# Row maxima from four partial products, two heads side by side in row groups of TensorE

## The reference, cut to what matters

```python
x_h = x.reshape(b, t, h, d).transpose(0, 2, 1, 3)            # 16, 16 heads, 512, 8
xw = jnp.einsum('bhtd,hde->bhte', x_h, w_att_val)
att = jnp.einsum('bhte,bhse->bhts', xw, x_h) / jnp.sqrt(jnp.asarray(d, x.dtype))
att = jax.nn.softmax(att, axis=-1)
vx = x @ wv_w.T + wv_b
...
o = jnp.einsum('bhts,bhsd->bhtd', att, vx)
return o @ out_w.T + out_b
```

## Time and profile before

| | us |
|---|---|
| median of 3 runs | 3337.77 (3323.8 to 3337.84) |
| the profiled execution | 3341.8 |
| its span | 3340.0 |
| PE, DVE, ACT, POOL busy | 3107.4, 2437.6, 2328.8, 1226.7 |

### The profile page before, as it was taken

How to read it: one execution, slowest core, us unless ns; L and a number is a source line. 1 busy time by engine, 2 the same in 40 slices (tenths; PEclk the granted TensorE clock), 3 DMA queues, 4 the chain that set the end, 5 groups by cost and what they waited for, 6 DMA issues and landing times.

```text
span 3340.0 us, 84102 instructions
## 1 busy us (share of the span) xinstructions
PE 3107.4 (93%) x34202; PEld 1889.6 (57%) x34202; DVE 2437.6 (73%) x4967; ACT 2328.8 (70%) x4800; POOL 1226.7 (37%) x778
## 2 busy tenths in 40 slices
PE   5899799999999999999999999999999999999976
PEld 5288446555565656465555656565555556565644
DVE  6722578878787868788787878788787878787643
ACT  4452376877777777868777776778787777777754
POOL 1133043444333333434433332434444333333433
PEclk9699699999999999999999999999999999999988
DMA  5356101011010111110100101111100101010000
GB/s 142 113 153 170 38 28 35 26 30 33 14 42 24 36 32 35 28 35 25 35 18 24 42 24 35 28 35 32 35 26 17 37 24 42 24 35 29 8 10 4
DMA packets 128413, 133.98 MB, mean 40 GB/s; under 512 B 18004, under 2 KB 110910, under 8 KB 128030
## 3 DMA queue, kind: packets, MB, share of 16 engines
q1 hardware_dynamic: 123488, 119.29, 12.9%
q0 software_dynamic: 4544, 9.32, 1.3%
HBM read 80.98 MB, written 30.28 MB: 33 GB/s over the span
## 4 chain that ended last, share of the span: by engine, by line
PE 65%; DVE 14%; ACT 7%; issue 3%; POOL 1%; DMA 1%; SPq 0%; POOLq 0%; ACTq 0%
PE bank L1456 7%; PE bank L2018 7%; PE bank L724 6%; PE bank L1469 6%; PE bank L1440 5%; PE bank L2062 3%; PE bank L2004 3%; PE bank L1994 3%; PE bank L1975 3%; PE bank L1960 2%; PE bank L1985 2%; PE bank L1717 2%; PE bank L2068 2%; DVE turn_f L2191 2%; PE bank L1735 2%
## 5 line engine op out<-in xcount | busy, mean ns | idle before, releaser
L1525 ACT ACTIVATE prob_a<-bank 128x512 f32<-128x512 f32 x1024 | 558.5, 605 | 132.0 <-PE bank L1469 129.4
L1580 DVE TENSOR_REDUCE nmax_a<-bank 128x1 f32<-128x512 f32 x768 | 496.8, 684 | 48.8 <-PE bank L1440 45.4
L1927 POOL TENSOR_TENSOR rn<-ss,minus_half 128x16 f32<-128x16 f32 x128 | 393.6, 3075 | 281.9 <-DVE ss L2186 278.7
L1950 POOL TENSOR_TENSOR rs_f<-rs_f,minus_half 128x4 f32<-128x4 f32 x32 | 33.0, 1032 | 1052.2 <-DVE rs_f L1320 1052.2
L1933 POOL TENSOR_TENSOR turn_f<-turn_f 128x512 f32<-128x512 f32 x256 | 325.3, 1291 | 203.1 <-DVE turn_f L2191 203.1
L2080 ACT ACTIVATE area<-bank 128x512 f32<-128x512 f32 x640 | 350.4, 603 | 55.7 <-PE bank L2018 46.3
L1469 PE MATMUL bank<-Qst_a,Kst_a 74*128 74x512 bf16 x1024 | 370.1, 386 | 9.3 <-DVE nmax_a L1580 5.8
L2191 DVE TENSOR_TENSOR turn_f<-area,rotf 128x1024 f32<-128x1024 f32 x256 | 303.7, 1218 | 7.8 <-POOL area L1937 6.8
L1440 PE MATMUL bank<-Kst_a,Qst_a 72*128 72x512 bf16 x768 | 298.6, 389 | 10.6 <-ACT prob_a L1525 6.2
L1456 PE MATMUL bank<-prob_a,V_a 128*9 128x512 f32 x2048 | 272.8, 605 | 18.1 <-ACT prob_a L1525 17.8
L1937 POOL TENSOR_TENSOR area<-turn_f,rn 128x1024 f32<-128x1024 f32 x128 | 243.9, 1905 | 18.4
(11 more groups left out here) (301 smaller groups left out, 6973.0 us busy)
## 6 DMA issues: line engine op xcount, KB each, us to landing
Qst_a<-dq_a SPq DMA_DIRECT2D x192, 96.0 KB
Kst_a<-dk_a SPq DMA_DIRECT2D x192, 96.0 KB
area<-in_W SPq DMA_DIRECT2D x25, 512.0 KB, 4.9
dq_a<-prob_a SPq DMA_DIRECT2D x80, 128.0 KB
V_f<-in_W SPq DMA_DIRECT2D x14, 512.0 KB, 4.5
dk_a<-prob_a SPq DMA_DIRECT2D x48, 128.0 KB
ys_d<-otok_f SPq DMA_DIRECT2D x39, 128.0 KB, 3.5
x_a<-in_x_in SPq DMA_DIRECT2D x16, 256.0 KB, 2.9
```

What stands on the lines that cost most here:

```text
L1525: nc.scalar.activation(dst, bk.full(act, product)[0:rows, :], func, **kw).then_inc(a_emptied["act"], 1)
L1580: nc.vector.tensor_reduce(out=nmax_a[:, g, t, j:j + 1], in_=bk.full(dve, f)[:], op=ALU.max, axis=AX.X, negate=True).then_inc(emptied, 1)
L1927: nc.gpsimd.tensor_tensor(rn[:, t % 2], ss[:, t % 2], minus_half[:], ALU.pow).then_inc(f_root, 1)
```

## The change

The first pass takes four of the nine partial products: the query's parts (1, 0, 0, 1) with the key's parts (0, 1, 0, 1), 4 x 8 = 32 rows. A stack `Qmx_a`, `Kmx_a` of its own holds the four heads of a group in four row groups of 32 partitions. `greatest` makes a head's product from its row group, and the products of two heads of the same quarter follow each other on PE, into two banks. The second pass keeps its 74 rows. To have the needed order of parts in DRAM, the spill writes 7 + 5 parts instead of 5 + 3; a stack is loaded by 8 DMAs instead of 6, two of 128 KB and six of 96 KB. The maxima's buffers become a ring of two, `mT_a` lies in unused rows of `Qst_a`, and four constants of the routing lie in buffers that are used later. The tables and the seats are all new.

```diff
+MT = 96
+Q_PARTS, K_PARTS = (1, 0, 0, 1, 2, 0, 1), (0, 1, 0, 1, 2)
...
-STEP = 178.7555
+STEP = 179.6323333
...
-        Kst_a, Qst_a = sb("Kst_a", [ROWS, RING, 4, T], BF16), sb("Qst_a", [ROWS, RING, 4, T], BF16)
+        Kst_a, Qst_a = sb("Kst_a", [ROWS, RING, 4, T], BF16), sb("Qst_a", [P, RING, 4, T], BF16)
+        Kmx_a, Qmx_a = sb("Kmx_a", [P, RING, T], BF16), sb("Qmx_a", [P, RING, T], BF16)
...
-        mhi_a, mT_a = sb("mhi_a", [P, G, NT, 4], BF16), sb("mT_a", [8, 2, T], BF16)
+        nmax_a, mparts_a = sb("nmax_a", [P, 2, NT, 4]), sb("mparts_a", [P, 2, NT, 2, 4])
+        mhi_a, mT_a = sb("mhi_a", [P, 2, NT, 4], BF16), Qst_a[MT:MT + 8, 0, 0:2, :]
...
-        first = [[("first", g, j, t) for j in range(4) for t in range(NT)] for g in range(G)]
+        first = [[("first", g, j, t) for t in range(NT) for j in range(4)] for g in range(G)]
...
-            for c in range(2 * SPLIT - 1):
-                sp.dma_start(dq[:, c], parts_q[:, c % SPLIT, :]).then_inc(s, 16)
-                if c < SPLIT:
-                    sp.dma_start(dk[:, c], parts_k[:, c, :]).then_inc(s, 16)
+            for c, part in enumerate(Q_PARTS):
+                sp.dma_start(dq[:, c], parts_q[:, part, :]).then_inc(s, 16)
+                if c < len(K_PARTS):
+                    sp.dma_start(dk[:, c], parts_k[:, K_PARTS[c], :]).then_inc(s, 16)
...
+            sp.dma_start(Qmx, dq[h:h + n, 0:4].rearrange("h c d t -> h (c d) t")).then_inc(s, 16)
+            sp.dma_start(Kmx, dk[h:h + n, 0:4].rearrange("h c d t -> h (c d) t")).then_inc(s, 16)
             rows = SPLIT * D0
-            q_rows, k_rows = (d[h:h + n].rearrange("h c d t -> (c d) h t") for d in (dq, dk))
+            q_rows, k_rows = (d[h:h + n, 2:].rearrange("h c d t -> (c d) h t") for d in (dq, dk))
...
+        def greatest(pe, bk, f):
+            _, g, j, t = f
+            rows = slice(32 * j, 32 * j + 32)
+            nc.tensor.matmul(bk.take(pe, f)[:], Qmx_a[rows, g % RING, t * P:(t + 1) * P],
+                             Kmx_a[rows, g % RING, :], start=True, stop=True).then_inc(a_filled, 1)
...
-                _, _, j, t = f = first[g][n]
                 if n == 0:
                     pe.wait_ge(*nth(r, a_stack[g], STACKED))
-                nc.tensor.matmul(bk.take(pe, f)[:], Qst_a[0:STACK, g % RING, j, t * P:(t + 1) * P],
-                                 Kst_a[0:STACK, g % RING, j, :], start=True, stop=True).then_inc(a_filled, 1)
+                for f in first[g][n:n + 2]:
+                    greatest(pe, bk, f)
```

More of the change, by code:

```diff
@@ L85 @@
                       314, 318.9, 323.8, 328.7, 333.6, 368.1),
[L86 to L92, removed]
+                     (-580.59649, -580.59449, -579.7103, -577.23387, -527.32015, -404.94056, -375.4343,
+                      -369.76896, 75.73973, 224.54907, 261.49146, 354.09913, 528.94049, 644.78191, 743.39294,
+                      842.14194, 907.68533, 1118.09809, 1131.5059, 1431.14303, 1431.14503, 1478.95922,
+                      1633.30607, 1659.50634, 1729.02134, 1732.58592, 1792.05439, 1792.15046, 1825.62492,
+                      1835.36098, 1849.53219, 1894.01227, 1915.99599, 1918.43704, 1929.50758, 1945.61039,
+                      1998.2619, 2003.15702, 2031.07034, 2071.21309, 2112.26554, 2133.72636, 2273.51371,
+                      2635.52919, 2639.14204, 2796.35045, 2864.13346, 4450.21639)),
             "head": ((1, 2),
-                     (94.66748, 95.66748))},
+                     (-257.83784, -256.83784))},
         "tensor": {
@@ L276 @@
                    17.8, 18.4, 18.8, 19.8, 23, 24),
[5 rows of a table removed]
-            "head": ((4.5, 6, 16, 16.7, 17.4, 18.1, 18.8, 19.5, 20.2, 20.9, 21.6, 22.3, 23, 23.7, 24.4, 25.1,
[4 rows of a table removed]
[5 rows of a table added]
+            "head": ((4.5, 6, 16, 17.4, 18.8, 20.2, 21.6, 23, 24.4, 25.8, 29),
[2 rows of a table added]
             "f": ((1, 1.3, 1.6, 6.4, 6.7, 7, 11, 11.2, 11.8, 12.1, 12.4, 13, 16.4, 16.5, 16.6, 16.8, 17.2,
@@ L424 @@
                    98.4, 99.6, 100.8, 102, 103.5, 105, 111),
[10 rows of a table removed]
[10 rows of a table added]
             "feed": ((6.55, 6.8, 7.1, 8.8, 9.3, 9.8, 10.725),
-                     (-112.76509, -111.65438, -110.77237, -103.08967, -101.79345, -99.4833, -77.78949)),
+                     (-110.64419, -110.64219, -109.49393, -102.26616, -99.67783, -95.92056, -78.05479)),
             "finish": ((13.2, 13.4, 13.6),
-                       (-58.22573, -55.4072, -53.6288))}}
+                       (-59.03677, -58.89768, -56.87055))}}
 SEATS = {
-    "a": ("154203542054415324103240512302323013124514003554035030102035022530543105243150130531013001"
-          "4532011520531051023103150350342"),
-    "b": "550243503111500034533453305032530452",
-    "head": "32010321541515105430",
-    "f": ("321401341540154325031214124541423451224254512415544510520151430123510545402503420312434212"
-          "4312012042141403"),
-    "feed": "433230540"}
+    "a": ("054132541354143251033504123003413054450230150440150122302414202014420325412305434035430410"
+          "4325142354530242105310210354410"),
+    "b": "525014251201105020322030345030052242",
+    "head": "12345034251432410244",
+    "f": ("351210451524013210142324355153521045121251224531441132103313510334530545243512543034030454"
+          "1254154011252523"),
+    "feed": "532523521"}
 B_AT = 5
@@ L749, in mixer_kernel @@
         turned_x = [hT_f[:], hT[:]]
-        tri, part_off = sb("tri", [P, P], BF16), sb("part_off", [P, 1])
-        block_at, ones_sq = sb("block_at", [P, NBLK]), sb("ones_sq", [P, P], BF16)
+        tri, part_off = gate_b[:].rearrange("p t g h -> p (t g h)")[:, 0:P // 2].bitcast(BF16), sb("part_off", [P, 1])
+        block_at, ones_sq = pool_b[:, 0:NBLK], gate_b[:].rearrange("p t g h -> p (t g h)")[:, P // 2:P].bitcast(BF16)
         m_stats = spare_b[:, 0:192].rearrange("p (g t s) -> p g t s", g=4, s=6)
@@ L943, in ranks @@
                 ps, first = rank_bank(c), 16 * c
-                nc.tensor.matmul(ps, tri[:], hot_bf[:, first:first + 16, :], start=True, stop=False, skip_group_check=True)
+                nc.tensor.matmul(ps, tri, hot_bf[:, first:first + 16, :], start=True, stop=False, skip_group_check=True)
                 for m in range(15):
-                    last = nc.tensor.matmul(ps[:, NX * (m + 1):].rearrange("p (n e) -> p n e", e=NX), ones_sq[:],
+                    last = nc.tensor.matmul(ps[:, NX * (m + 1):].rearrange("p (n e) -> p n e", e=NX), ones_sq,
                                             hot_bf[:, first + m:first + m + 1, :].to_broadcast([P, 15 - m, NX]),
@@ L970, in open_tensor @@
             for c in range(4):
-                last = nc.tensor.matmul(banks[5][:, NX * c:NX * (c + 1)], ones_sq[:], m_held[:, c, :], start=True, stop=True)
+                last = nc.tensor.matmul(banks[5][:, NX * c:NX * (c + 1)], ones_sq, m_held[:, c, :], start=True, stop=True)
             last.then_inc(m_ranks, 1)
@@ L1267, in mixer_kernel @@
         f_tanh, f_out, f_stored = sem("f_tanh"), sem("f_out"), sem("f_stored")
-        first = [[("first", g, j, t) for j in range(4) for t in range(NT)] for g in range(G)]
+        first = [[("first", g, j, t) for t in range(NT) for j in range(4)] for g in range(G)]
         second = [[("second", g, k, j) for k in range(NT) for j in range(4)] for g in range(G)]
         plan_head = [(4.5, "xnT", ["act"]), (6, "xw", ["act"]), (6, "v", ["dve"])]
-        plan_head += [(16 + 0.7 * n, f, ["dve"]) for n, f in enumerate(first[0])] + [(29, ("mT", 0), ["act"])]
+        plan_head += [(16 + 0.7 * (n - n % 2), f, ["dve"]) for n, f in enumerate(first[0])] + [(29, ("mT", 0), ["act"])]
         plan_a = []
@@ L1278, in mixer_kernel @@
             for n in range(16):
-                if g + 1 < G:
-                    plan_a.append((A_GROUP[g] + 1.2 * n, first[g + 1][n], ["dve"]))
+                if g + 1 < G and n % 2 == 0:
+                    plan_a += [(A_GROUP[g] + 1.2 * n, f, ["dve"]) for f in first[g + 1][n:n + 2]]
                 plan_a.append((A_GROUP[g] + 1.2 * n + 0.4, second[g][n], ["act"]))
@@ L1378, in a_stack_load @@
         def a_stack_load(sp, g):
-            load_stack(sp, dq_a, dk_a, 4 * g, 4, Qst_a[:, g % RING], Kst_a[:, g % RING], a_stack[g])
+            load_stack(sp, dq_a, dk_a, 4 * g, 4, Qst_a[:, g % RING], Kst_a[:, g % RING], Qmx_a[:, g % RING], Kmx_a[:, g % RING], a_stack[g])
         def head_sync(r, sp, bk, b, after_body, attended):
@@ L1422, in head_tensor @@
             last.then_inc(a_filled, 1)
-            for n, f in enumerate(first[0]):
-                _, _, j, t = f
+            for n in range(0, 16, 2):
                 yield 16 + 0.7 * n
@@ L1427, in head_tensor @@
                     pe.wait_ge(*nth(r, a_stack[0], STACKED))
-                nc.tensor.matmul(bk.take(pe, f)[:], Qst_a[0:STACK, 0, j, t * P:(t + 1) * P],
-                                 Kst_a[0:STACK, 0, j, :], start=True, stop=True).then_inc(a_filled, 1)
```

(18 more changed lines are left out.)

50 lines of the change are left out of this document (25 added, 25 removed), and 422 rows, old and new, of tables (OPEN, TIMES).

## The result

| | us |
|---|---|
| before, median of 4 runs beside it | 3337.81 (3323.8 to 3343.74) |
| after, median of 4 runs | 3683.83 (3679.03 to 3686.4) |
| ratio | 1.1053, 95% interval 1.1028 to 1.1078 |
| span of the profiled execution, clock | 3684.6, 0.919 |

Slower by a tenth: 346 us, outside the range of 3292 to 3392. By the "xw" products (L1421 now) a repeat takes 204.8 us (1195.5 to 1400.3) against 182.8, and the opening, from the first "xw" to the second, 332.0 against 301.5. The opening is 30.5 us longer and the rest of the profiled execution 314, which is 21 us for each of the 15 repeats.

The account below looks back on a forecast made before the run. PE was taken to bound the kernel. Terms summed to -0.2 us a repeat, -3 over 15, and +3 in the opening, so gain and loss cancel: 3338 us, with a range of 3292 to 3392.

Parts of the forecast that it names:

- What bounds it: Whole repeat: PE bounds it, with some 177.6 us of its own work in 182.8; nothing else comes near.
- Part 1: First-pass row-maximum matmuls: pairs run side by side, so half leave PE's line; -7.0 us a repeat, +0.2 for issue.
- rival C: First-pass pairs don't run side by side, yet tiling switches are paid; +102 us, 3440 us; chance 0.05.
- Part 2: PE's order: tiling changes 149 times a repeat instead of 102, 0.092 us each; +4.3 us a repeat.
- Part 3: Head of the repeat: first stack lands 3.4 to 3.9 us later; new PE wait taken as 1.0 us, at most 2.7.
- Part 4: Later stacks: two more loads delay them; +0.8 us for the last group, +0.2 for the one before, bounds 0 to 1.5 each.
- Part 5: Redrawn timetables and moved buffers: order priced at 0 (-2 to +2), shared buffers 0, odd PE stalls +0.3 us a repeat.
- Rival B: Head's stack wait: from about 1.5 us the clock falls, in perhaps half the repeats; +57 us, 3395 us; chance 0.18.
- Opening: Before the repeats: PE's 9.08 us wait for the first stack grows by 3.9, partly taken back; +3 us (0 to 8).

Follow-up runs that it names:

- g3: Changed kernel with the DMA work and full-height first pass of the kernel before, leaving the new order, seats and buffers; 3394.54 us, ratio 1.0186.
- g1: g3 with all twelve parts spilled; 3412.66 us, ratio 1.0243.
- g2: g1 with the first pass in pairs of 32-row products on rows already there (other products than the reference's), no added loads; 3407.74 us, ratio 1.0217.
- e1: Changed kernel, but the two added loads each read one contiguous piece of 128 rows (not the right rows); 3471.84 us, ratio 1.0373.
- e3_even_split: Changed kernel with the even loads of e1 (not the right rows) and the first pass waiting for them alone; 3420.32 us, ratio 1.0208.
- f3: e1 with full-height first-pass products; the added loads, on a semaphore of their own, are still waited for but not read; 3503.31 us, ratio 1.0447.
- e2: Changed kernel, loads unchanged, but the two added ones have their own semaphore and the first pass waits for them alone; 3566.85 us, ratio 1.0666.
- e4: Changed kernel with the added loads made as eight DMAs of 32 right rows, the first pass waiting for these alone; 3519.21 us, ratio 1.0505.
- i1_row_on_act: e3_even_split with the row of maxima of groups 1 to 3 sent from ACT's queue instead of SP's; 3425.24 us, ratio 1.0242.
- f4_one_load_each_head: e4 with Q's and K's parts side by side in one scratch tensor, so four DMAs of 32 rows of 2 KB; 3424.11 us, ratio 1.0213.

## Why the prediction was wrong

How the loss of 0.105 comes together, each line from the ratios above (times 3338 us; they add up to 351, where the medians differ by 346):

| step | ratio to before | its part, us |
|---|---|---|
| order, seats and buffers (g3) | 1.0186 | +62 |
| four more spills (g1) | 1.0243 | +19 |
| pairs (g2) | 1.0217 | -9 (g1 and g2 not told apart) |
| two even loads a stack (e1) | 1.0373 | +52 |
| the added loads with 4 heads outermost (after) | 1.1053 | +227 |

The 52 us are in the main the price of waiting for them with the whole stack, not of moving them: e3_even_split moves the same bytes, waits for these loads alone, and stands at 1.0208, where g2_pairs_no_loads without them has 1.0217.

**What bounds it: right.** DVE and ACT do the same work in a repeat as before, and the 12.8 us that PE newly waits are the largest part of the 22 us that a repeat gained.

**Part 1, right.** The pairs run side by side; rival C is out.

**Part 2, right in kind.** Forecast -2.5 us a repeat for both parts. Measured -1.3 to -2.2 (g2 against g1 at full clock), and 25 us in all, or some 1.7 a repeat (f3 against e1).

**Part 3, the step that failed.** It priced the two added loads by their issue, "at the spill's pace they are +1.3 us". An issue takes 0.57 to 0.59 us indeed, but the stack lands 4.3 us later behind its first load (6.4 and 10.7 us, by the completion records), and e1_even shows why: it is the form of the loads, 4 heads outermost. From the first spill to the first product are 22.1 us (1220.01 to 1242.08) and were 15.0 (1473.79 to 1488.82), so 7.0 more, or at least that, since PE had no wait before; forecast was a stack 3.4 to 3.9 us later. For the landing the form is nearly all that was missing: with even loads the same distance is 18.5 us (e1_even, whose spill begins at 1540.90), 3.5 more. The wait at the head was taken as 1.0 us with 2.7 as its upper end, and was 5.52.

**Part 4, the same error.** +1.0 for both later stacks, bounds 1.5 each; measured 2.95 + 4.34 = 7.3 us. That the second pass can come to wait for the row of maxima behind the loads was seen rightly (60.3 and 62.2 us in e2 and e4); in the changed kernel itself the first pass's wait comes first, and no such wait is left.

**Part 5, wrong by itself.** The redraw was put at 0, at most 2. It costs 3.1 us a repeat (185.9 against 182.8) and 12 in the opening, and g3 doesn't tell the order from the moved buffers, which were put at 0 too. Comparing counts and shapes of instructions could not show it. PE is busy 178.3 us where it was 177.2, and idle 7.6 instead of 5.8, in waits of 0.2 to 0.5 us. Which moves do it stays open; the old order with pairs was not run.

**Rival B's clock falls came, in more places than it said, but as the smaller part.** The clock does fall in or behind the new waits: from 1.00 to 0.53 on the mean of 1239 to 1250, that is to 1.2 GHz for nearly all of it. It falls at all three stalls of a repeat, not behind one in half of them, some 24 us a repeat. Of the 22 us that a repeat gained, 12.8 are waits, 3.1 the order and -1.3 the pairs; the 7.4 left I put down to the clock, by difference. B was priced at 57 us, since the wait was thought to be 2 us once. Its 1.5 us are not borne out: 1.94 us in e1_even has a fall behind it, but so has a wait of 1.2 us at the same place in g1_order_and_spills, while 1.3 us elsewhere has none. The trace of the kernel before could have said so: a wait of 1.51 us at 1304.83 has no fall behind it, and one of 1.35 us at 2044.91 has one of 10 us. The length of one wait does not decide it alone; what else does stays open.

**Opening.** Forecast +3 (0 to 8), measured +30.5: 12 with the order alone (g3), 19 when the spills are added (g1), still 19 with pairs and even loads (e1), and 30.5 with the uneven ones. PE's wait for the first stack grew by 9.9 us, from 9.08 to 19.0, where 3.9 was forecast; all these are single traces.

**Chances.** 0.33 stood on slower, and no rival was priced above 3440. The bounds of the wait were drawn from loads of another form; for an operation whose form the trace doesn't show, the end of the range should have been its bytes on the fewest engines it can have.

**Open.** Why even loads that PE does not wait for (e3_even_split) leave the second pass waiting for ACT, 1.3 us a repeat, which g2_pairs_no_loads has not; i1_row_on_act did not take it away. No version here beats the kernel before. The best that makes the 32-row products of the right rows, f4_one_load_each_head, gets four fifths of the loss back (0.084 of 0.105), and g3_order_only, which has none of them, stands at 1.0186.

## What to carry to other kernels

Price a DMA by its form and not by its bytes or its issue: look what stands outermost on both sides (here 4 heads against 128 partitions), and write it so that 32 or 128 rows stand there on both. A transfer that nothing waited for before is now in front of the first matmul of a stage, so ask for its landing, and give a consumer a semaphore for just what it reads. A new order of a tuned kernel is an edit with a price of its own; run it alone.
